# Adjacency mask of a graph-attention and mixture-of-experts stack: cast and transposed by DMA, with all of the first chunk's indicator quads scaled by ScalarE

## The reference, cut to what matters

```python
x = x + _L0_gnn_ref(_layernorm(x), adj, ...)    # 4 heads, softmax over the neighbours of each node
x = x + _L0_ffn_ref(_layernorm(x), ...)         # 8 experts, 2 of them weighted per node
x = x + _L1_gnn_ref(_layernorm(x), adj, ...)    # scores averaged over 4 heads, one softmax
x = x + _L1_ffn_ref(_layernorm(x), ...)         # routed layers

# the first graph layer
Wh = (h @ W.T + b).reshape(N, H, D)
e = leaky_relu(src[:, None, :] + dst[None, :, :], 0.2)
att = softmax(where(adj[:, :, None] == 1, e, -9e15), axis=1)
h_prime = einsum('ijh,jhd->ihd', att, Wh)
```

## Time and profile before

| what | value |
|---|---|
| median of 3 runs | 620.15 us (620.02 to 620.75) |
| profiled execution | 619.58 us |
| its span, first to last instruction | 617.6 us |
| mean granted TensorE clock | 0.944 of full |
| busy, share of the span | TensorE 88%, VectorE 83%, ScalarE 60%, GpSimd 26% |

### The profile page before, as it was taken

The page is one execution under the profiler, slowest core; times in us unless marked ns, Lnnn a source line. Parts: engine busy times, 40 slices in busy tenths (PEclk is TensorE's granted clock), DMA queues, the critical chain, the costliest instruction groups (busy, mean ns, idle before and its releaser), DMA issues.

```text
span 617.6 us, 13265 instructions
## 1 busy us (share of the span) xinstructions
PE 542.4 (88%) x5098; PEld 431.8 (70%) x5098; DVE 513.4 (83%) x903; ACT 371.6 (60%) x752; POOL 162.5 (26%) x162
## 2 busy tenths in 40 slices
PE   2879787999999999999989797999996856889987
PEld 1668784979777877878668484588786646567865
DVE  6799999997789968799678648899999998997550
ACT  1699795758887687788574826733421401556565
POOL 3311110075211426641523010121315000183320
PEclk9989896989999899999999898999999878789999
DMA  6485940022165299986897023020202944474663
GB/s 137 94 167 110 242 114 2 18 88 70 39 201 205 72 260 261 263 167 143 149 192 119 18 90 118 2 69 0 69 1 67 313 130 127 120 211 146 191 185 104
DMA packets 50632, 78.32 MB, mean 127 GB/s; under 512 B 5470, under 2 KB 26902, under 8 KB 50570
## 3 DMA queue, kind: packets, MB, share of 16 engines
q1 hardware_dynamic: 32810, 53.03, 27.4%
q0 software_dynamic: 15168, 20.97, 20.5%
q10 hardware_dynamic: 2592, 3.48, 2.3%
HBM read 80.57 MB, written 22.06 MB: 166 GB/s over the span
## 4 chain that ended last, share of the span: by engine, by line
PE 55%; DVE 30%; ACT 8%; issue 5%; DMA 1%; ACTq 0%; POOL 0%; POOLq 0%; SPq 0%; DVEq 0%
DVE arena L1657 16%; PE bank L702 13%; PE bank L714 13%; PE bank L630 12%; PE bank L873 4%; DVE arena L1479 3%; ACT arena L1153 2%; PE bank L830 2%; PE bank L913 2%; DVE arena L1483 1%; PE bank L579 1%; PE bank L606 1%; PE bank L814 1%; PE bank L884 1%; DMA x<-in_x 1%
## 5 line engine op out<-in xcount | busy, mean ns | idle before, releaser
L501 POOL TENSOR_TENSOR x<-x,ysb 128x512 f32<-128x512 f32 x36 | 64.2, 1782 | 268.7 <-ACT ysb L1105 257.5
L1153 ACT ACTIVATE arena<-heads,nd 128x512 bf16<-128x512 f32 x176 | 111.9, 720 | 24.4 <-PE bank L630 24.1
L702 PE MATMUL bank<-hTc,arena 128*128 128x512 f32 x192 | 91.2, 629 | 5.6 <-ACT reg_c L1094 5.6
L1657 DVE SCALAR_TENSOR_TENSOR arena<-reg_b,nd,arena 128x1536 f32<-128x1536 f32 x48 | 92.0, 1977 | 0.0
L714 PEld LDWEIGHTS bank<-arena,reg_c 128*128 128x128 f32 x768 | 87.7, 192 | 4.8 <-issue 4.7
L714 PE MATMUL bank<-arena,reg_c 128*128 128x128 f32 x768 | 88.8, 275 | 0.0
L1094 ACT ACTIVATE reg_c<-bank,b 128x512 f32<-128x512 f32 x96 | 65.3, 687 | 20.1 <-PE bank L702 20.1
L630 PEld LDWEIGHTS bank<-reg_b,arena 128*128 128x128 bf16 x1536 | 73.7, 100 | 3.1 <-issue 3.0
L630 PE MATMUL bank<-reg_b,arena 128*128 128x99 bf16 x1536 | 74.7, 211 | 0.0
L1105 ACT ACTIVATE ysb<-bank,comb 128x128 f32<-128x128 f32 x128 | 36.6, 368 | 60.7 <-PE bank L922 39.9
L702 PEld LDWEIGHTS bank<-hTc,arena 128*128 128x128 f32 x192 | 37.5, 202 | 50.0 <-issue 41.6
(11 more groups left out here) (196 smaller groups left out, 838.0 us busy)
## 6 DMA issues: line engine op xcount, KB each, us to landing
maskT<-routed_sums SPq DMA_DIRECT2D x48, 256.0 KB, 3.1
reg_c<-in_adj POOLq DMA_DIRECT2D x16, 512.0 KB, 7.3
arena<-in_w1T SPq DMA_DIRECT2D x16, 512.0 KB, 4.0
arena<-in_w2T SPq DMA_DIRECT2D x16, 512.0 KB, 6.4
routed_sums<-in_wsT SPq DMA_DIRECT2D x32, 256.0 KB, 8.6
routed_sums<-in_wrT POOLq DMA_DIRECT2D x32, 256.0 KB, 11.0
arena<-routed_sums SPq DMA_DIRECT2D x32, 256.0 KB, 3.0
routed_sums<-ident POOLq DMA_DIRECT2D x4, 1024.0 KB, 12.8
```

The costliest lines, as they stand in the source:

```text
L501: nc.gpsimd.tensor_tensor(xi, xi, ysb[:, e % 3, :].rearrange("p (t d) -> p t d", d=P), ALU.add).then_inc(s_acc, 1)
L702: mm(bank[b][:, :], w1[:, s, e % 2, c * P:(c + 1) * P], hTc[:, :], start=True, stop=True).then_inc(full[b], 1)
L1153: last = af(ind[:, q, b, j, :], sbc[:, h, :], ACT.Relu, bias=nd[:, q * QT + j, h:h + 1], scale=BIG)
L1657: last = v.scalar_tensor_tensor(p, row, nd[:, t, h:h + 1], p if h else maskT[:, t, columns], ALU.max, ALU.mult)
```

## The change

1. The cast goes from adj to a new DRAM tensor `mask_rows` (rows 4,352 bytes apart), issued by GpSimd (`cast_rows`), and SP issues for each row block one transposing DMA from there into `maskT` (`transpose_rows`). The transposes on TensorE, their PSUM copies on ScalarE, `adj` and `identb` are gone. Four semaphores count the casts (r mod 4) and four the transposes; a cast of block r from 4 on waits for the transpose of block r - 4.
2. Casts 0 to 3 are where the loads were, 4 to 11 follow GpSimd's reduction, 12 to 15 sit in its loop over the expert outputs. SP issues transposes 0 to 7 ahead of the store of the source scores, 8 to 11 after the second pair of expert weights and the bias loads, 12 and 13 after the third pair, 14 and 15 after the fourth.
3. All four quads of each head of chunk 0 are scaled by ScalarE and finished by one VectorE minimum.
4. `attend_first` alternates between banks 0, 1 and 6, 7, and `attend_whole` between banks 2 and 3.
5. The source rows of chunk 1 are broadcast on GpSimd's queue instead of ScalarE's, with semaphores of their own (`s_row1`).

The diff, cut to its core (declarations, counts of semaphore values and renamed arguments are left out):

```diff
+        mask_rows = nc.dram_tensor("mask_rows", (N, N + P), BF16, kind="Internal").ap()
...
+        def mask_ready(engine, c):
+
+            for r in range(CT):
+                engine.wait_ge(s_mask[r], 16 * (c + 1))
...
+            def transpose_rows(rows):
+
+                for r in rows:
+                    sp.wait_ge(s_cast[r % 4], 16 * (r // 4 + 1))
+                    sp.dma_start(maskT[:, :, r * P:(r + 1) * P], mask_rows[r * P:(r + 1) * P, 0:N],
+                                 transpose=True).then_inc(s_mask[r % CT], 16)
+
+            transpose_rows(range(2 * CT))
             sp.wait_ge(ev["score"], 1)
...
+                if h == 2:
+                    transpose_rows(range(3 * CT, 3 * CT + 2))
...
+                    transpose_rows(range(2 * CT, 3 * CT))
+            transpose_rows(range(3 * CT + 2, T))
...
-            def load_rows(r):
-                if r >= 4:
-                    pool.wait_ge(full[5 if r % 2 else 7], (r - 4) // 2 + 1 + (0 if r % 2 else H // 2))
-                pool.dma_start(adj[:, r % 4, :], a["adj"][r * P:(r + 1) * P, :]).then_inc(s_adj[r % 4], 16)
+            def cast_rows(r):
+
+                rows = slice(r * P, (r + 1) * P)
+                if r >= CT:
+
+                    pool.wait_ge(s_mask[r % CT], 16 * (r // CT))
+                pool.dma_start(mask_rows[rows, 0:N], a["adj"][rows, :]).then_inc(s_cast[r % 4], 16)
...
-            for r in range(4, T):
-                load_rows(r)
+            for r in range(CT, 3 * CT):
+                cast_rows(r)
...
+            pool.wait_ge(s_spill, 16 * (C - 1))
+            for h in range(H):
+
+                pool.wait_ge(s_above, Q * (h + 1))
+                pool.dma_start(sbc[:, h, :], later_rows[0, h:h + 1, :].to_broadcast([P, CW])).then_inc(s_row1[h], 16)
...
                 pool.wait_ge(ev["y"], n + 1)
+                if n < CT:
+                    cast_rows(3 * CT + n)
...
-                use(0, "att")
-                use(1, "att")
+                first = h % 2 * 6
+                use(first, "att")
+                use(first + 1, "att")
...
-            for r in range(CT):
-                mask_rows(r)
-            pe.wait_ge(ev["mask"], 2 * CT)
+            mask_ready(pe, 0)
             attend_whole(0)
-            mask_rows(CT)
...
-            for r in range(CT):
-                mask_rows(r)
             for h in range(2):
-                for q in (2, 3):
+                for q in range(Q):
                     above(h, h, q)
-            mask_rows(CT)
...
+                quads = range(Q) if h < 2 else range(1, 2) if h == 2 else range(2, Q)
+                for q in quads:
+                    above(min(h + 2, H), (h + 2) % H if h < H - 1 else 0, q)
...
-                    if q < 2:
-                        if h >= 2:
-
-                            dve.wait_ge(s_indf, (h - 2) * (Q - 1) + q + 1)
-                        for j in range(QT):
-                            t = q * QT + j
-                            last = v.scalar_tensor_tensor(to[:, j, :], sbc[:, h, :], thr[:, t, h:h + 1],
-                                                          maskT[:, t, 0:CW], ALU.is_gt, ALU.mult)
-                    else:
-                        dve.wait_ge(s_above, 2 * h + q - 1)
-                        last = v.tensor_tensor(to, maskT[:, q * QT:(q + 1) * QT, 0:CW], to, ALU.min)
-                    last.then_inc(s_ind, 1)
+                    dve.wait_ge(s_above, h * Q + q + 1)
+                    v.tensor_tensor(to, maskT[:, q * QT:(q + 1) * QT, 0:CW], to, ALU.min).then_inc(s_ind, 1)
...
             dve.wait_ge(ev["rows"], H)
-            dve.wait_ge(ev["mask"], 2 * CT)
+            mask_ready(dve, 0)
```

More of the change, by code:

```diff
@@ L175, in gnn_moe_stack @@
         nd = sb("nd", [P, T, H])
-        thr = sb("thr", [P, 2 * QT, H])
+        thr = sb("thr", [P, QT, H])
         dsh = sb("dsh", [P, T, H])
@@ L584, in normalised @@
                 pe.wait_ge(ev["hTc"], k.at("hTc"))
[L586 to L595, removed]
             def project(s, c, banks=(2, 3)):
@@ L664, in attend_first @@
                             if t == T - 1 and i % 2:
-                                last.then_inc(full[i // 2], 1)
+                                last.then_inc(full[first + i // 2], 1)
                     if q < Q - 1:
@@ L1015, in ln_out @@
                    ACT.Copy).then_inc(ev["hTc"], 1)
-            def mask_rows(r):
-                for half in range(2):
-                    b = MASK_BANKS[r % 2][half]
-                    got(b)
-                    af(maskT[:, half * 8:(half + 1) * 8, r * P:(r + 1) * P],
-                       bankb[b].rearrange("p (j i) -> p j i", i=P), ACT.Copy).then_inc(ev["mask"], 1)
             def project(whx, c, banks=(2, 3)):
@@ L1048, in whole_sums, with sums @@
                     act.wait_ge(s_attf, v)
-                got(2)
-                af(whole, bank[2][:, 0:CT * VW], ACT.Copy).then_inc(ev["att"], 1)
-            def sums(*widths, to=att):
+                got(b)
+                af(whole, bank[b][:, 0:CT * VW], ACT.Copy).then_inc(ev["att"], 1)
+            def sums(*widths, to=att, first=0):
                 v = k.event("sums") - 1
@@ L1057, in sums @@
                 o = 0
-                for b, w in enumerate(widths):
+                for b, w in enumerate(widths, first):
                     got(b)
@@ L1162, in head @@
                 if c == 0:
[L1163 to L1171 removed]
+                    whole_sums(2 + h % 2)
+                sums(4 * VW, 4 * VW, first=0 if c else h % 2 * 6)
+                if 0 < c < C - 1:
+                    act.dma_start(sbc[:, h, :], later_rows[c, h:h + 1, :].to_broadcast([P, CW])).then_inc(s_row[h], 16)
             for h in range(2):
[L1173 removed]
+                for q in range(Q):
                     above(h, h, q)
[L1175 removed]
             act.wait_ge(s_xb, C)
@@ L1179, in _ @@
                 head(0, h)
-                if h == 2:
-                    act.wait_ge(s_u, H)
-                rows = list(ROWS[h])
-                if h == H - 1:
-                    above(H, 0, 3)
-                quads = ((2, 3), (2, 3), (1, 2), ())[h]
-                for j in range(3):
-                    if h == 0 and j == 2:
-                        got(4)
-                        for c in range(1, C):
-                            part = slice((c - 1) * GRP, (c - 1) * GRP + H)
-                            last = af(hTc[part, :], bank[4][part, :], ACT.Copy)
-                        last.then_inc(ev["score"], 1)
-                    for q in quads[j:j + 1]:
-                        above(h + 2, (h + 2) % H, q)
-                    for r in rows[j:j + 1]:
-                        mask_rows(r)
+                quads = range(Q) if h < 2 else range(1, 2) if h == 2 else range(2, Q)
+                for q in quads:
+                    above(min(h + 2, H), (h + 2) % H if h < H - 1 else 0, q)
+                if h == 0:
+                    got(4)
+                    for c in range(1, C):
+                        part = slice((c - 1) * GRP, (c - 1) * GRP + H)
+                        last = af(hTc[part, :], bank[4][part, :], ACT.Copy)
+                    last.then_inc(ev["score"], 1)
             act.wait_ge(s_w2, 16 * NW2)
@@ L1496, in indicate @@
                         elif n == H:
-                            dve.wait_ge(full[1], n)
+                            dve.wait_ge(*attended(n - 1))
                         last = v.tensor_tensor(ind[:, q, 0, :, :], maskT[:, q * QT:(q + 1) * QT, cs],
@@ L1520, in _ @@
             then(v.tensor_tensor(nd[:, :, :], D0, bsum[:, :].unsqueeze(1).to_broadcast([P, T, H]), ALU.add))
-            then(v.tensor_scalar(thr[:, :, :], nd[:, 0:2 * QT, :], -1.0, None, ALU.mult))
+            then(v.tensor_scalar(thr[:, :, :], nd[:, 0:QT, :], -1.0, None, ALU.mult))
             then(v.tensor_scalar(nd[:, :, :], nd[:, :, :], BIG, None, ALU.mult))
@@ L1624, in _ @@
                 norm(c - 1, c - 1 + C)
-                dve.wait_ge(ev["mask"], c * 2 * CT + 2 * CT)
+                mask_ready(dve, c)
                 indicate(c, 0, range(2))
```

65 lines of the change are left out of this document (31 added, 34 removed).

## The result

The changed kernel took 613.27 us (median of 4 executions, 610.44 to 615.36), the kernel before 620.45 us beside it (620.02 to 621.55). The ratio is 0.9873 with an interval of 0.9842 to 0.9904: 7.2 us faster. A repeat later gave 614.36 against 621.04 us, ratio 0.9896 (0.9847 to 0.9945). The forecast was 610.7 us, likeliest range 607 to 613, so sign and size hold; the median is 2.6 us above the number and 0.3 us above that range. The profiled execution of after was the slowest of its four, 615.36 us with a span of 613.5; beside the profiled one of before (619.58 us) that is only 4.2 us less. What follows compares these two traces, so it explains 4.2 us; the changed kernel's own executions are 5 us apart.

The account below looks back on a forecast made before the run. VectorE was taken to bound the kernel until 96.44 us. Its 12.4 us less some 3 for TensorE gave 9.4: 619.58 became 610.2, and with the median 0.57 above, 610.7 us; likeliest range 607 to 613.

Parts of the forecast that it names:

- VectorE, -12.4 us: First query chunk: a head's four quads take 4.54 us instead of 7.65, saving 12.4 us over four heads.
- ScalarE feeds the quads: ScalarE drops 30.3 us of mask copies, gains eight quads at 2.48 us each, costs VectorE under 1 us.
- TensorE takes 3 us back: End of the stage: `attend_first(2)` takes 7.4 us and TensorE's products return some 3 of VectorE's 12.4 us.
- The layout of the stage: Engine-by-engine schedule from 28.66 us: first quad at 38.7, merge 3 at 79.9 instead of 89.34 us, 9.4 us earlier.
- The mask, hidden: First four transposes land by 32 to 37 us, before VectorE asks at 38.7, so no wait shows.
- X: Price of one DMA transpose of a 0.524 MB mask row block, taken as 2 us.
- one or two casts slipping in (2.5 us each): Casts running among the first four transposes move the mask's landing from 32 to 37 us.
- late transposes, part of the gain eaten: Rival: a transpose price of 2.4 to 4.8 us on shared engines makes VectorE wait; 611 to 620 us, chance 0.11.
- GpSimd's reduction unchanged: GpSimd's reduction stays at 26.35 us, with cast 4 following it.
- The row of chunk 1 at 68 us: GpSimd's broadcast source row lands at 68 us, before ScalarE asks at 73.8, with 3.6 us to land.
- Slow transposes: Rival: `mask_ready(dve, 0)` ends last, from 4.8 us a transpose (or 8); slower than before, chance 0.20.
- The ceiling of 12.4 us: Rival: all of VectorE's 12.4 us arrive, 607 us; chance 0.60 counted together with the forecast.

Follow-up runs that it names:

- e5: Kernel before with all four quads of each chunk 0 head scaled by ScalarE, TensorE's mask transposes and ScalarE's copies kept; 634.59 us, ratio 1.0219.
- e1: Changed kernel with casts 4 and later issued only once the first four transposes have landed; 613.08 us, ratio 0.9889.
- e6: As e1, with casts 8 to 11 issued only behind the chunk 1 source-row broadcasts for heads 0 to 2; 611.38 us, ratio 0.9875.
- e12: As e8, but with the first transpose ahead of GpSimd's reduction; 609.82 us, ratio 0.9847.
- e2: Changed kernel with plain transfers of the same bytes and pieces instead of transposing ones, mask left untransposed; 612.57 us, one execution.
- e7: Changed kernel with casts 8 to 11 behind the chunk 1 source-row broadcasts for heads 0 to 2, without e1's wait; 612.43 us, ratio 0.9897.
- e8: As e6, with SP holding the first transpose until GpSimd's reduction is done; 607.60 us, ratio 0.9803.
- e10: The changed kernel run again, unaltered; 614.36 us, ratio 0.9896.
- e11: The kernel of e8 run again, on the same chip as the changed kernel; 609.29 us, ratio 0.9803.
- e4: Changed kernel with the first two quads of each chunk 0 head made by VectorE's compares as before; 620.97 us, ratio 1.0003.
- e9: As e8, plus 64 and 128 TensorE products that nothing reads, to keep TensorE from idling; 611.46 us, ratio 0.9858.
- e3: Changed kernel with each cast issued as four transfers of 512 columns; 615.90 us, ratio 0.9923.

## Why the prediction was right, point by point

- **VectorE, -12.4 us: right.** 4.63 us a head instead of 4.54.
- **ScalarE feeds the quads: right.** 2.46 us a quad against 2.48. That the 30 us of copies had to go first, e5 shows: 13.5 us slower without that.
- **TensorE takes 3 us back: right where VectorE is in time, absent in after.** 7.88, 7.84 and 7.28 us for `attend_first(2)` in e1, e6 and e12 against the 7.4 taken. In after the late mask had pushed the heads together, the product took 5.64, and 1.8 us of the lateness was paid back.
- **The layout of the stage: right, and better shown by its terms than by its total.** Put the measured start of the first quad (for 38.7) and the measured `attend_first(2)` (for 7.4) into the sum, and merge 3 comes out within 0.2 us in e2, e6, e7, e8, e10, e11 and e12. In e12, where both are nearest to what was laid out (39.69 and 7.28 us), it gives 80.8 against 80.66. That e8 and e11 hit 79.9 (79.46 and 79.67) is chance: there the quad is 1.4 to 1.6 us too late and the product 1.8 us too short.
- **The mask, hidden: wrong, and the step of the sum that was mis-sized.** X was taken as 2 us; alone it is 2.2 to 2.9 us (e8). That would still have been hidden: with casts 4 and later held back the four were in by 34.03 us (e1). The step that failed is "one or two casts slipping in (2.5 us each)". They don't add their own time, they all but stop the transposes: landing at 44.5 instead of 32 to 37, VectorE 6.0 us late. This is the rival *late transposes, part of the gain eaten*, to which I gave 0.11, by another mechanism than a large X; 613.27 lies in its 611 to 620, and 0.3 us above the likeliest case's 607 to 613. That the median came so near is in part luck: the late mask was half hidden by the faster product, and in other executions it was less late (42.9 us in e10).
- **GpSimd's reduction unchanged: wrong by 1.3 us.** 27.68 instead of 26.35 in after, 26.82 in e8 where the transposes are held back. Why they delay it stays open.
- **The row of chunk 1 at 68 us: wrong by 13.** It came at 81.0. ScalarE's scores, expected at 61.4, left SP at 67.87 (the late mask's 6 us); the store took 4.57 us and the broadcast 7.62, where I had 3.6 for the latter by the earlier trace rows. ScalarE waited 1.0 us for it in after and 5.6 us in e1, as the place named among the signs of "wrong" has it; by the sum above, 0.7 and 2.2 us of that reached merge 3.
- **The sum for this trace.** From 79.9: mask +6.0 (which holds the 1.3 of the reduction), TensorE -1.8, row up to +1.0: 84.1 to 85.1; measured 84.87. So 5.0 us were missing at merge 3, and the profiled execution was 5.2 us above its own forecast of 610.2.
- **Rivals that fell.** Slow transposes: X is far from 4.8. The reading of 1309 ns a tile one after another, that is 21 us, is excluded by e8's 2.8. The ceiling of 12.4 us wasn't reached by after; e8's kernel came near it (13.1 and 11.7 us by medians) with merge 3 only 9.9 us earlier, the rest lies in the spread of the part behind. From the first expert product on the time is as before (517.4 against 517.1 us), and the 4.5 us arrive as 4.1.

What stays open: why the part behind the first expert product differs by up to 5 us between kernels that are the same there, and when transpose 3 lands in executions that weren't profiled. The two further banks and the move of the broadcasts to GpSimd's queue, which the forecast put at nothing, were never tried apart; e4 has both, and gained nothing.

## What to carry to other kernels

Where a chain of small transfers has a deadline, look at what else the same program puts on the DMA engines in that time: a large transfer that nobody waits for yet can stop it almost wholly. Holding it back by one wait brought the small ones in 10 us sooner, but everything behind it in the same queue moves back too: in e1 the source row did, and the time stayed. Whether the lateness costs anything is a second question; in e7 no cost could be seen. When a repaired wait doesn't move the time, read the same engines again for the next thing that was just as late; here that was the row behind the casts, then TensorE's product at the lower clock. And check the terms when a total fits: e8's did with two of them off. And where two engines share the work of a stage, try each half of an exchange alone: each was worth nothing or a loss, and only both together paid.

## What the runs showed of the hardware

- A DMA transpose of 128 rows of 2048 bf16 (0.524 MB) goes every 2.25 to 2.85 us from issue to issue when alone (e8), 184 to 233 GB/s. The Trainium skill has 261 GB/s for it (DMA: Bandwidth & Descriptors, Latency and other measured facts). These runs are below that.
- Beside a single stream of casts in 3.7 KB pieces, the transposes fell from 0.47 MB to 0.03 MB in 2 us (after), though the DMA engines as a whole still moved 187 GB/s. Plain transfers in pieces of the same size fell from 0.44 to 0.02 MB (e2).
- GpSimd's reduction over partitions, whose operand VectorE writes, starts later when transfers into `maskT` are in flight. From the end of VectorE's instruction that writes its operand to its start it took 1.7 to 2.6 us in the kernels with the old mask path or with the transposes held back (before, e5, e8, e9, e11), and 2.9 to 4.4 us with transposes or plain transfers under way (after, e10, e1, e2, e4, e6, e7), and 5.7 in e3 with its small casts; e12, with one transpose ahead of it, took 2.6. What delays it wasn't tried apart.
- TensorE ran the 64 products of `attend_first(2)` in 5.63 to 5.64 us after 0.81 to 1.77 us of idle time (e7, e10, after, e11, e8) and in 7.28 to 8.51 us after 2.44 to 6.55 us (e12, before, e6, e1, e3, e2, e4). From 64 to 68 us the granted clock was 0.50 in e1, the lower of its two levels (1.2 GHz), and 1.00 in e8. So a VectorE that started later could end the stage sooner: e8, 0.9 us late for the mask, had merge 3 at 79.46 us, and e12, with no wait, at 80.66.
